# Moving two weight loads and the embedding products within the first four turns of a two-layer attention kernel

## What is computed

```python
xn = layernorm(x)
q, k, v = xn @ Wq + bq, xn @ Wk + bk, xn @ Wv + bv
y = attention(q, k, v)                     # softmax over the keys in layer 0, "linear" in layer 1
scale, shift = split(silu(cond) @ emb_w + emb_b)
h = layernorm(y) * (1 + scale) + shift
x = x + silu(h) @ out_w + out_b
```

## Time and profile before

| What | Value |
|---|---|
| Median of 3 runs | 897.81 us |
| The profiled execution, its own time | 897.78 us |
| Its span | 895.9 us |
| PE busy | 863.7 us, 96% of the span |
| DVE busy | 763.3 us, 85% |
| ACT busy | 670.7 us, 75% |
| POOL busy | 614.8 us, 69% |
| Chain that ended last, PE's share | 89% |
| Granted TensorE clock | 1.00 |

### The profile page before, as it was taken

How to read it: one execution, slowest core, us unless ns; L and a number is a source line. 1 busy time by engine, 2 the same in 40 slices (tenths; PEclk the granted TensorE clock), 3 DMA queues, 4 the chain that set the end, 5 groups by cost and what they waited for, 6 DMA issues and landing times.

```text
span 895.9 us, 23751 instructions
## 1 busy us (share of the span) xinstructions
PE 863.7 (96%) x8432; PEld 718.3 (80%) x8432; DVE 763.3 (85%) x1573; ACT 670.7 (75%) x1202; POOL 614.8 (69%) x1095
## 2 busy tenths in 40 slices
PE   5899999999999999999999898999999999999996
PEld 4677777777777777777776567999999999999996
DVE  5789999999999999999998657788888888888875
ACT  2257777777777777677767777888888888888875
POOL 3456575756666666657574347888888888888875
PEclk9999999999999999999999999999999999999999
DMA  8862535343434434343433223122222222223101
GB/s 258 257 197 106 179 114 184 114 169 129 166 132 153 145 139 159 136 156 142 149 129 134 93 71 116 38 88 87 85 88 86 87 89 87 87 84 87 37 31 59
DMA packets 77412, 108.54 MB, mean 121 GB/s; under 512 B 7088, under 2 KB 43408, under 8 KB 77168
## 3 DMA queue, kind: packets, MB, share of 16 engines
q1 hardware_dynamic: 77296, 107.03, 35.3%
HBM read 35.60 MB, written 16.88 MB: 59 GB/s over the span
## 4 chain that ended last, share of the span: by engine, by line
PE 89%; DVE 3%; issue 3%; ACT 2%; POOL 1%; SPq 0%; DMA 0%; DVEq 0%; ACTq 0%; POOLq 0%
PE psX L1312 16%; PE psY L1427 13%; PE psT L1312 9%; PE psM L1312 9%; PE psT L1408 6%; PE psT L1389 5%; PE psY L1312 5%; PE psT L1592 3%; PE psM L1408 3%; PE psT L1323 3%; PE psY L1542 3%; PE psY L1448 3%; PE psM L1323 3%; PE psM L1389 2%; PE psX L1460 2%
## 5 line engine op out<-in xcount | busy, mean ns | idle before, releaser
L976 DVE TENSOR_REDUCE sb_cm<-psT 128x4 f32<-128x1024 f32 x168 | 202.4, 1215 | 12.3 <-PE psT L1408 12.1
L591 ACT ACTIVATE sb_P<-psT 128x1024 f32<-128x1024 f32 x176 | 177.7, 1026 | 30.0 <-PE psT L1389 14.5
L1427 PE MATMUL psY<-sb_P,sb_Vp 128*17 128x256 f32 x2048 | 129.2, 381 | 1.0 <-DVE sb_yr L1002 0.7
L976 DVE TENSOR_REDUCE sb_cm<-psM 128x4 f32<-128x1024 f32 x88 | 107.0, 1216 | 7.7 <-PE psM L1408 7.7
L404 POOL TENSOR_SCALAR sb_ve<-sb_mv 128x2 f32<-128x2 f32 x32 | 7.3, 229 | 134.1 <-DVE sb_mv L1010 134.1
L1312 PE MATMUL psX<-sb_xT,sb_W0h 128*128 128x256 f32 x488 | 93.7, 294 | 0.0
L591 ACT ACTIVATE sb_P<-psM 128x1024 f32<-128x1024 f32 x80 | 82.0, 1025 | 14.4 <-PE psM L1389 6.7
L1427 PEld LDWEIGHTS psY<-sb_P,sb_Vp 128*17 128x17 f32 x2048 | 50.6, 97 | 46.8 <-issue 6.1
L421 POOL TENSOR_TENSOR sb_qp<-sb_qp 128x512 fp32r<-128x512 f32 x64 | 82.1, 1282 | 5.3
L1408 PE MATMUL psT<-sb_Ks,sb_Qs 64*128 64x256 f32 x672 | 74.7, 305 | 2.7 <-DVE sb_cm L976 1.9
L1389 PE MATMUL psT<-sb_Qs,sb_Ks 64*128 64x256 f32 x704 | 74.5, 295 | 1.9 <-ACT sb_P L591 1.9
(11 more groups left out here) (199 smaller groups left out, 2581.6 us busy)
## 6 DMA issues: line engine op xcount, KB each, us to landing
sb_Qs<-sb_qp SPq DMA_DIRECT2D x96, 256.0 KB
sb_Ks<-sb_qp SPq DMA_DIRECT2D x96, 256.0 KB
sb_xt<-in_x SPq DMA_DIRECT2D x32, 256.0 KB, 3.0
y_normed<-sb_Yn SPq DMA_DIRECT2D x32, 256.0 KB, 2.0
sb_u<-in_x SPq DMA_DIRECT2D x32, 256.0 KB, 2.9
sb_u<-y_normed SPq DMA_DIRECT2D x32, 256.0 KB, 3.0
out<-sb_v SPq DMA_DIRECT2D x31, 256.0 KB, 2.2
sb_v<-key_mask SPq DMA_DIRECT2D x32, 128.0 KB, 3.5
```

Of the source, the lines that this page charges most:

```text
L591: a.activation(P[G % 4][:, :], pairs[place["S", n, g][0]][:, :], ACT.Exp).then_inc(s_ex, 1)
L976: v.tensor_reduce(cm[n % 2][:, 4 * j:4 * j + 4], scores, AX.X, ALU.max, negate=True).then_inc(s_mx, 1)
L1427: ins = pe.matmul(psY[32 * j:32 * j + 17, y0:y0 + T], Vp[n % RING][:, m, 4 * gr + j, :], Pj[:, c0:c0 + 256], start=(m == 0), stop=(m == 1))
```

## The change

`EW` is loaded at the end of SP's turn 0, behind `filled(1)`; `others()` moves to the end of SP's turn 1, behind `filled(2)`, and the wait for the key mask's DMA from turn 2 to turn 3. On PE step 0 moves behind the q product of turn 2, step 1 behind the k product of turn 2, step 2 to the end of turn 2 without its column; step 3 stays behind `xturn(3)` and takes the column that step 2 had; its own column becomes step 5, behind the q product of turn 3. The wait for `s_ld[3]` stands in step 4. ACT's copies follow: `embedded(0)` and `embedded(1)` behind the q and the k of turn 2, `gathered()` behind the q of turn 3.

```diff
 # SP
             filled(0)
-            sp.wait_ge(s_lw[2], 16)
-            sp.dma_start(EW[:, :, :, :], emb).then_inc(s_ld[2], 16)
...
                 if t + 1 < RING:
                     filled(t + 1)
                 if t == 0:
+                    sp.dma_start(EW[:, :, :, :], emb).then_inc(s_ld[2], 16)
+                if t == 1:
                     others()
-                if t == 2:
+                if t == 3:
                     sp.wait_ge(s_md, 32)
 # ACT
-                if t == 2:
-                    embedded(1)
-                if t == 3:
-                    gathered()
...
                     qk(t, 0)
+                if t == 2:
+                    embedded(0)
+                if t == 3:
+                    gathered()
...
                     qk(t, 1)
+                if t == 2:
+                    embedded(1)
                 exps(t, 6)
...
                 exps(t, 7)
-                if t == 1:
-                    embedded(0)
 # PE, embeddings(step)
                 elif step == 2:
-                    pe.wait_ge(s_ld[3], 16 * LOADS[3])
                     pe.wait_ge(p_act, 5)
                     pe.wait_ge(p_sum, 1)
                     gather(0)
-                    column(psT[0][:, 256:258], 1, 1)
                 elif step == 3:
                     pe.wait_ge(p_act, 6)
                     gather(1)
+                    column(psT[0][:, 256:258], 1, 1)
+                elif step == 5:
                     column(psT[0][:, 258:260], 1, 2).then_inc(p_pe, 1)
                 else:
+                    pe.wait_ge(s_ld[3], 16 * LOADS[3])
                     pe.wait_ge(p_act, 6)
                     row(psT[0][:, 512:768], 1, 0).then_inc(p_pe, 1)
 # PE, the turns
                     xturn(t)
-                if t == 2:
-                    embeddings(1)
                 if t == 3:
                     embeddings(3)
...
                 if t == 2:
-                    embeddings(2)
+                    embeddings(0)
+                if t == 3:
+                    embeddings(5)
                 scores(t, 3)
...
                 if t in RAMP:
                     qk(t, 1)
+                if t == 2:
+                    embeddings(1)
                 rowmax(t, 5)
...
                     yturn(t - 4, 1)
-                if t == 1:
-                    embeddings(0)
                 if t == 2:
+                    embeddings(2)
                     embeddings(4)
```

## The result

The changed kernel takes 903.80 us (median of three, 902.88 to 903.84) against 897.81: 1.0055 times the kernel before, interval 1.0036 to 1.0075. That is 6.0 us slower, in the forecast direction, more than the forecast 3.5 and 0.9 above the top of its range. A later set of five runs gave 902.84 and 1.0043 (1.0030 to 1.0056), just inside the range. The profiled execution is one of 903.80, its span 901.8.

The account below looks back on a forecast made before the run. PE was taken to bound the kernel, carrying turn 4's delay to the end: +2.4 for the row's wait, +1.2 in turn 3, less 0.1 for overlaps, is +3.5 on 897.8, so 901.3 us; range 897.4 to 902.9.

Parts of the forecast that it names:

- PE bounds from turn 4 on, and a delay is carried one to one.: From turn 4 PE has no slack, so any shift of its start, now 59.77 us, reaches the end in full.
- The 0.8 us ahead of batch 0's first maximum go.: PE's 0.82 us wait at 26.52 goes once EW no longer lies ahead of batch 0's copies; gain 0 to 0.8.
- EW lands at 34.9.: EW, issued at 23.44 behind filled(1), takes 11.5 us and lands at 34.9.
- The last Wo lands at 47.4.: Last load of others(), behind filled(2): lands at 47.4, bounds 44.0 to 48.6, taken from the earlier sequence.
- The Trainium skill's 341 GB/s: First rival: at this rate others() lands at 42.7, before PE asks, so no wait at the row; chance 0.21.
- is covered by the larger wait below: Turn 2: step 0's wait for EW, 0 to 1 us, counts nothing because PE waits longer at the row.
- Worse: Rival: longer queue, EW late, pushing batch 1's copies and the fills; landing 48.6, +5.1 to 5.5, 903; chance 0.03.
- Faster: Rival: queue relief frees the score operands' copies, loads land before 43.4; -2.2, 895.6 us; chance 0.09.
- Steps 0 and 1 only change places.: Turn 2: moving both steps costs PE nothing; idle time at their old places is won back further on.
- Turn 3: +1.2.: Turn 3: step 5's column and the wait for ACT's copies, less 0.2 that DVE gives back; +1.2.
- a forecast +1.4: Turn 3: first scores starts later by 0.9 for the column and 0.5 for ACT's copies; bounds 0.9 to 1.7.
- +2.4 for a wait at the row: End of turn 2: PE waits until 47.4 for the late loads; turn 3's first maximum at 48.4 instead of 46.01.

Follow-up runs that it names:

- e1: The change with EW's load put back ahead of turn 0, so only others() is moved late; 906.05 us, ratio 1.0094.
- h1: e1 with separate semaphores for W1 and the bias rows, so that the row step waits for W1 alone; 900.34 us, ratio 1.0019.
- e2: The change with both loads back in their old places, the new order on PE and ACT kept; 901.24 us, ratio 1.0045.
- k4: The kernel before with separate semaphores for W1 and the bias rows, and diag and Wo loads moved to SP's turn 4; 898.05 us, ratio 0.9992.
- k2: The change with separate semaphores for W1 and the bias rows, so that the row waits for W1 alone; 902.75 us, ratio 1.0040.
- k1: The changed kernel run once more, unaltered; 902.84 us, ratio 1.0043.
- k3: k2 with 20 transposes that nobody reads ahead of turn 2's k product; 901.72 us, ratio 1.0031.

## Why the prediction was right or wrong

- *PE bounds from turn 4 on, and a delay is carried one to one.* Right: turn 4 +5.85, span +5.9.
- *The 0.8 us ahead of batch 0's first maximum go.* Right in the change, but that EW caused them is not shown: with EW at its old place the wait is 0.50 (e1), 0.84 (h1), 1.26 (e2) and none at all (k4). Turn 2 began 1.98 us earlier: the wait, step 0's 1.0, and 0.3 that turn 1 was ahead already (21.36 against 21.63), which no part of the change explains.
- *EW lands at 34.9.* It landed at 34.7. *The last Wo lands at 47.4.* 47.8. Taking the landing from the same sequence behind the same fill pair worked to half a microsecond. The Trainium skill's 341 GB/s ("DMA: Bandwidth & Descriptors", "Bandwidth") would have had it at an estimated 42.7, and no run shows that. The two figures that the prediction took from that row don't agree with each other: 1 MB in 6.15 us is 170 GB/s, and by that time an estimate for the 1856 KB is 11.1 us, landing at 48.2, close to what was measured.
- ***A wait at EW "is covered by the larger wait below".*** This is the step that failed. The prediction asked only when EW's own reader, step 0, would need it. What lay behind EW in the queue, batch 1's q copies, its sum took as unchanged because SP issues them at the same time. The rival "Worse" (0.03) did have EW push batch 1's copies, but only as a delay of the fills and so of the last landing, and "Faster" had read ACT's wait for that very buffer (37.40). The copies landed for ACT at 39.0 instead of 37.4, and PE, 1.7 to 2 us earlier in the turn, waited 3.3 us where it had not waited before. The larger wait at the row was never larger in the change: PE came 1.8 us after the landing. It is real (3.8 us in e1) but hidden: taking it away in k2 changed the median by 0.09 us.
- *The clock.* The prediction didn't mention it. In the half-clock stretch 5.88 us were spent on 3.30 us of work: +2.6, about what the result exceeds the forecast by. The amount differs between executions (1.4 us in k2), so how near the measured time comes to the range is partly chance: the 902.84 of the later set lies within it, with the same wrong mechanism.
- *"Steps 0 and 1 only change places."* Put at nothing, but turn 2's +0.7 and h1's turns 1 and 2 (0.3 us gained where 0.95 left) show that it wasn't, and e2, the order alone, took 3.9 us more than the kernel before.
- *Turn 3: +1.2.* Measured +1.23 (and 14.3 us in e2, k1, k2 and k3 too, whenever the clock was full): `scores` started 6.32 us behind the turn's transposes against 4.90 in the earlier trace rows, +1.42 against a forecast +1.4. In turn 3 the mechanism was as forecast, a column and a wait for ACT's copies. That it can be had back was not shown.
- *The Trainium skill's rule to issue early and wait late* ("DMA: Bandwidth & Descriptors", "Rules for kernel authors") bears on it: the trace agrees for `others()`, as e1 and h1 show. For EW the harm was to the DMAs behind it and not to its own reader, a case that the rule doesn't name.

So the direction was right, and of the two terms of the sum the first, +2.4 for a wait at the row, came from another place and was +4.6 (the maximum behind the row at 50.63 instead of 46.01). That the direction came out is partly luck: the wait that was to bring it hardly occurs in the change.

One thing stays open: why EW (2048 KB) held batch 1's q copies until 39.0 where `others()` (1856 KB), issued at the same place, let them land by 37.4. The 192 KB alone don't explain 1.6 us.

## What to carry to other kernels

When a load is moved, list not only who waits for it but every DMA that is issued behind it before it has landed, and who waits for those; here EW held up batch 1's q copies (39.0 in the change, in time for 35.3 in e1) and `others()` those of batch 2 (h1). When one wait is taken away, price the next one behind it in the same list, since waits in series only show one at a time. A load that several steps share should not make the first of them wait for the last piece: its own semaphore for W1 took the ratio from 1.009 (e1) to 1.002 (h1), though in the change, where another wait hid this one, it gave nothing (k2). Test the parts of a change alone, too: the new order without the moved loads (e2) lost as much as the whole, and no profile of the whole could say so.

## What the runs showed of the hardware

PE's clock fell to its half level in the ramp not only behind waits of 3.3 and 3.8 us: in e2_order_only no single wait ahead of the fall was over 1.4 us. The kernel before has it too in part of its executions: in the second set 14 of 30 have a mean clock of 0.999 or 1.000 and take 896.67 to 897.82 us, the other 16 are at 0.994 to 0.998 and take 898.56 to 902.26. So the spread of a kernel's times here goes with its clock. Where the half clock lay in those executions no profile shows; in every profile of this study that has one, it lies in the first 67 us. And 20 transposes that nobody reads, placed in a wait (k3_row_w1_filled), made a kernel about 1 us faster.
